# A gated cross-attention block with routed experts: the projections before the attention loop are derived in another way and spread differently over the engines

## The chip, the cores and the metric

The kernel runs on one core of a Trainium2 chip. The metric is the device time of one execution in microseconds (us); of several executions the median counts. The core has five engines with a queue each, which meet only at semaphores: PE (TensorE, products and transposes), DVE (VectorE), ACT (ScalarE), POOL (GpSimd) and SP (SyncE, which here only starts transfers). ACT and POOL start transfers too.

## The reference

`x` has 4 sequences of 1024 tokens of 256 values, the context has 77 keys for each sequence. Cut to what matters:

```python
def proj(x): return (x @ W1.T + b1) @ W2.T + b2
q  = proj(layernorm(x)); k = proj(ctx)
a  = softmax(q @ k.T / sqrt(256) + mask) @ ctx
x  = x + tanh(g_xattn) * a
h  = layernorm(x); route = softmax(h @ router_w + router_b)
e  = argmax(route)                       # one of 8 experts for each token
y  = (silu(h @ w1a[e]) * (h @ w1g[e])) @ w2[e]
x  = x + tanh(g_ffn) * max(route) * y
```

## The kernel before, in words

The tokens are taken in 8 groups (`NG`) of 4 x 128 (group g holds 128 tokens of each sequence, b = 0 to 3). There are three stages.

Preparation (to about 23 us). Both projections have no nonlinearity between their layers, so their product M = W2 W1 is formed once. `w2_t` is W2 transposed by PE (L973) and copied by DVE (L695). PE forms M transposed (`ps_p`, L993), which ACT copies to `m_t` (L541); `kp_t`, the projected keys, is M times the transposed context plus the bias `bq` (L1008; ACT adds the bias for one half at L553, DVE for the other at L720). The queries are never projected: the keys are multiplied by M once more (L1025, `keys_t`), so that the scores are raw tokens times `keys_t`. The layer norm's mean is taken off by using `m_c`, M with the mean over its input dimension removed. Before the change `m_c` is formed by a product of its own, W2 times the mean-free W1: DVE makes `w1_c` (L697 to L701), PE multiplies (L1014), DVE copies (L726). Then come `keys_t` (scaled by ACT at L556 and by DVE at L729), the bias row `bias_c` (product L1030, scaled by DVE at L732) and `values`, the context times tanh of the gate (DVE, L723). The norm's 1/deviation comes from `bn_stats` and `bn_aggr` on DVE (L687, L691: `stats1(g)`) and a power on POOL (L389, L390: `norm1`).

Attention loop. In round i each engine goes through a list written by hand: PE the scores of group i (L1049), the transposes of the tokens of group i+1 (L965), of the probabilities of group i-1 (L1039), and the attention products of group i-2 (L1058); ACT the copy of the transposed tokens (`copy_xt`, L548), the copy of the probabilities (L570), the exponentials (L579) and half a piece of expert 0's weights rounded to `w_hi` (L564); DVE mask and maximum (L749 to L755), the sum into `x_all` (L769), the second statistics (L778, L784) and `stats1(5 + i)` for i up to 2; POOL the masks (L400), `norm1`, `norm2` (L409 to L419) and the rest `w_lo` (L426). Then the tokens are sorted by expert (L812 to L1106), with a few unused products (L1104) among the PE work.

Expert loop (from about 96 us on). 36 tiles or so of 128 sorted tokens; PE multiplies with the weights split into two parts (L1127, L1137, L1145), three products each.

SP's queue: the weights, the context, 8 groups of `x`, then the three pieces of expert 0's weights into `staging`, piece k waiting until piece k-1 has landed (L328), then the rows of each finished group (L336), and so on. `m_t` and `m_c` share memory with `x_t[:, 1]`, which `copy_xt(1)` overwrites.

Of the kernel before, what the change touches and what calls it, by code (L numbers as in the profile page):

```python
# [20 lines left out]
ALU = mybir.AluOpType  # L21
# [3 lines left out]
P = 128  # L25


def flamingo_block(nc, x, ctx_kv, mask, g_xattn, g_ffn, w1, b1, w2, b2, router_w, router_b, e_w1, e_w2, out):
# [27 lines left out]
    UNUSED = (2, 2, 11)  # L56
    FIRST = 4
# [16 lines left out]
    with ExitStack() as top:  # L74
# [68 lines left out]
        w1_in, w2_in, w1_c, w2_t = (sb0(name, [P, DC, D]) for name in ("w1_in", "w2_in", "w1_c", "w2_t"))  # L143
        w1_mean = sb0("w1_mean", [P, 2, DC])
# [88 lines left out]
        w1c_step = sem("w1c_step")  # L233
# [12 lines left out]
        vr_ready = sem("vr_ready")  # L246
        bn1_ready = sem("bn1_ready")
# [62 lines left out]
        EARLY = 5  # L310
        QUARTERS = 4
# [7 lines left out]
        def _(sp):  # L319
# [36 lines left out]
        def _(pool):  # L356
# [28 lines left out]
            def norm1(first_group, end_group):  # L385
                n = (end_group - first_group) * B
                at = slice(first_group, end_group)
                pool.wait_ge(mv1_ready, end_group)
                link(nc.gpsimd.tensor_scalar(var_eps1[:, at], mv1[:, at, :, 1], EPS, None, ALU.add))  # L389
# [135 lines left out]
        def _(act):  # L525
# [13 lines left out]
            nc.scalar.activation(tanh_g[:], gates_in[:], ACT.Tanh).then_inc(tanh_ready, 1)  # L539
            act.wait_ge(m_psum, 1)  # L540
            nc.scalar.copy(m_t[:], ps_p[:].rearrange("p (c d) -> p c d", c=DC)).then_inc(mt_ready, 1)  # L541

            def copy_xt(g):
# [3 lines left out]
                for k in range(DC):  # L547
# [7 lines left out]
            act.wait_ge(keys_psum, 1)  # L555
            nc.scalar.mul(keys_t[:, 0, :, 0:KEYS], ps_p[:, 0:KB].rearrange("p (b k) -> p b k", b=B), SCALE  # L556
                          ).then_inc(keys_ready, 1)
# [123 lines left out]
        def _(dve):  # L681


            def stats1(g):
                dve.wait_ge(x_loaded[g], 16)
# [3 lines left out]
                dve.wait_ge(bn1_ready, g + 1)  # L689
                for b in range(B):  # L690
# [5 lines left out]
            dve.wait_ge(w1_loaded, 16)  # L696
            nc.vector.tensor_reduce(w1_mean[:, 0], w1_in[:], AX.X, ALU.add).then_inc(w1c_step, 1)  # L697
            dve.wait_ge(w1c_step, 1)
            nc.vector.tensor_scalar(w1_mean[:, 1], w1_mean[:, 0], 1.0 / D, None, ALU.mult).then_inc(w1c_step, 1)
            dve.wait_ge(w1c_step, 2)  # L700
            nc.vector.tensor_tensor(out=w1_c[:], in0=w1_in[:], in1=w1_mean[:, 1].unsqueeze(2).to_broadcast([P, DC, D]),  # L701
                                    op=ALU.subtract).then_inc(w1c_step, 1)
# [10 lines left out]
            stats1(1)  # L713
# [7 lines left out]
            dve.wait_ge(tanh_ready, 1)  # L721
            dve.wait_ge(ctx_loaded, 16)
# [5 lines left out]
            dve.wait_ge(keys_psum, 1)  # L728
            nc.vector.tensor_scalar(keys_t[:, 1, :, 0:KEYS], ps_o[1][:, 0:KB].rearrange("p (b k) -> p b k", b=B), SCALE,  # L729
                                    None, ALU.mult).then_inc(keys_ready, 1)  # L730
            dve.wait_ge(bias_psum, 1)
            nc.vector.tensor_scalar(bias_c[:], ps_s[1][:, 0:KB], SCALE, None, ALU.mult).then_inc(bias_ready, 1)  # L732
            stats1(4)

# [5 lines left out]
            def mask_and_max(g):  # L740
# [6 lines left out]
                dve.wait_ge(rstd1_ready, g + 1)  # L747
# [208 lines left out]
        def _(pe):  # L956
# [12 lines left out]
            pe.wait_ge(consts_ready, 1)  # L969
            pe.wait_ge(w2_loaded, 16)  # L970
# [4 lines left out]
            last.then_inc(w2t_psum, 1)  # L975
            pe.wait_ge(ctx_loaded, 16)
# [25 lines left out]

            for k in range(DC):
                pe.wait_ge(ctxt_ready[k], 1)
            pe.wait_ge(mt_ready, 1)
# [5 lines left out]
            pe.wait_ge(w1c_step, 3)  # L1011
# [15 lines left out]
            last.then_inc(keys_psum, 1)  # L1027
# [185 lines left out]
```

## Time and profile before

| | |
|---|---|
| three executions | 441.12, 441.44 (median), 442.80 us |
| the profiled execution | 444.54 us |
| its span, first to last instruction | 442.7 us |
| PE busy | 405.9 us (92%) |
| POOL busy | 241.8 us (55%) |
| DVE busy | 214.5 us (48%) |
| ACT busy | 180.6 us (41%) |

The profile is of one execution; its times count from the first instruction. A row of the timeline has the start, the duration of the group (from the start of its first to the end of its last instruction, both in us), the engine, the line, what is written and read, the shape and the number of instructions; in brackets how long the engine had been idle before and what ended that. The chain of waits is followed back from the last instruction. PE shows a float product as two instructions (two passes).

### The profile page before, as it was taken

What the parts mean: (1) busy time and instruction counts of PE and PEld (TensorE: products, weight loads), DVE (VectorE), ACT (ScalarE), POOL (GpSimd) and SP (SyncE); (2) the same over time, 40 slices, a digit from 0 to 9 for tenths busy, and PEclk for the clock granted to TensorE, in tenths of its full rate; (3) what the DMA queues carried; (4) which work ended last, traced back from release to release, by engine and by line L of the source; (5) the groups of instructions that cost most, each with busy time, mean ns of one, the idle gap of its engine ahead of it and who ended that gap; (6) DMA issues with size and microseconds to landing.
All of it is one profiled execution on the core that took longest, in us unless ns stands there. A gap on an engine that the chain in (4) does not pass through costs nothing.

```text
span 442.7 us, 9878 instructions
## 1 busy us (share of the span) xinstructions
PE 405.9 (92%) x2446; PEld 350.5 (79%) x2447; DVE 214.5 (48%) x520; ACT 180.6 (41%) x356; POOL 241.8 (55%) x323
## 2 busy tenths in 40 slices
PE   5998986289899999999999999999999999999990
PEld 4787874157788888888888888888888888888880
DVE  3789898934444434444334344334344434444340
ACT  1167654025443645445523245345433643233230
POOL 2356996224763787877772267738842686222231
PEclk9999895589999999999999999999999999999997
DMA  7941224825324243334440004423331000000100
GB/s 202 358 147 66 96 98 143 98 70 204 122 116 131 80 168 114 119 119 130 182 159 27 24 17 133 163 78 119 119 121 34 13 32 31 24 24 28 24 24 23
DMA packets 29850, 44.01 MB, mean 99 GB/s; under 512 B 8377, under 2 KB 25581, under 8 KB 27791
## 3 DMA queue, kind: packets, MB, share of 16 engines
q1 hardware_dynamic: 24095, 34.45, 23.9%
q0 software_dynamic: 3456, 9.11, 6.3%
q10 hardware_dynamic: 2288, 0.33, 0.5%
q8 instruction: 4, 0.07, 0.1%
q14 instruction: 7, 0.06, 0.0%
HBM read 35.44 MB, written 8.83 MB: 100 GB/s over the span
## 4 chain that ended last, share of the span: by engine, by line
PE 82%; POOL 6%; DVE 5%; DMA 2%; issue 2%; ACT 1%; DVEq 0%; POOLq 0%; SPq 0%; ACTq 0%
PE py L1145 22%; PE pa L1127 22%; PE pg L1127 22%; PE ph L1137 7%; POOL w_lo L426 2%; PE px L1112 2%; PE ps_s L1049 1%; PE ps_o L1058 1%; POOL rstd L410 1%; DMA ctx_in<-in_ctx 1%; PE ps_p L993 1%; PE ps_xt L965 1%; DVE x_norm L903 1%; DMA x_sorted<-residual_rows,idx_gather 1%; DVE x_all L769 1%
## 5 line engine op out<-in xcount | busy, mean ns | idle before, releaser
L920 DVE TENSOR_TENSOR ht_lo<-ph,ht_hi 128x512 fp32r<-128x512 f32 x70 | 48.4, 692 | 135.4 <-ACT ht_hi L651 135.4
L497 POOL TENSOR_TENSOR w_lo<-staging,w_hi x84 | 107.1, 1304 | 6.7 <-ACT w_hi L672 4.0
L651 ACT CAST ht_hi<-ph 128x512 fp32r<-128x512 f32 x70 | 41.1, 587 | 120.7 <-PE ph L1137 85.5
L1145 PE MATMUL py<-w_hi,ht_hi 128*128 x272 | 79.0, 291 | 0.0
L1145 PE MATMUL py<-w_lo,ht_hi 128*128 x272 | 76.2, 280 | 0.0
L1145 PE MATMUL py<-w_hi,ht_lo 128*128 x272 | 76.2, 280 | 0.0
L486 POOL DMA_INDIRECT out<-out_tile,idx_now x34 | 34.7, 1019 | 72.8 <-DVE out_tile L928 72.2
L1127 PE MATMUL pa<-w_hi,xt_hi 128*128 (+1 forms) x140 | 58.2, 416 | 0.8 <-ACT xt_hi L633 0.8
L453 POOL DMA_INDIRECT x_sorted<-residual_rows,idx_now x34 | 35.6, 1048 | 39.6 <-DVE x_norm L903 21.5
L1127 PE MATMUL pg<-w_lo,xt_hi 128*128 (+1 forms) x140 | 55.4, 396 | 0.0
L1127 PE MATMUL pg<-w_hi,xt_lo 128*128 (+1 forms) x140 | 55.4, 396 | 0.0
L1127 PE MATMUL pg<-w_hi,xt_hi 128*128 (+1 forms) x140 | 55.4, 395 | 0.0
L1127 PE MATMUL pa<-w_hi,xt_lo 128*128 (+1 forms) x140 | 55.3, 395 | 0.0
L1127 PE MATMUL pa<-w_lo,xt_hi 128*128 (+1 forms) x140 | 55.3, 395 | 0.0
L1145 PEld LDWEIGHTS py<-w_lo,ht_hi 128*128 128x128 f32 x272 | 52.0, 191 | 0.0
L915 DVE TENSOR_TENSOR hidden<-pg,silu 128x512 f32<-128x512 f32 x70 | 48.1, 686 | 6.6 <-ACT silu L645 3.4
L1145 PEld LDWEIGHTS py<-w_hi,ht_hi 128*128 128x128 f32 x272 | 51.1, 188 | 0.0
L1145 PEld LDWEIGHTS py<-w_hi,ht_lo 128*128 128x128 f32 x272 | 51.1, 188 | 0.0
L672 ACT CAST w_hi<-staging x21 | 40.1, 1912 | 9.8 <-PE py L1145 7.9
L645 ACT ACTIVATE silu<-pa 128x512 f32<-128x512 f32 x70 | 42.3, 604 | 1.9 <-PE pg L1127 1.9
L1137 PE MATMUL ph<-ident,hidden 128*128 128x128 f32 x280 | 41.9, 272 | 0.0
L633 ACT CAST xt_hi<-px 128x256 fp32r<-128x256 f32 x36 | 13.4, 372 | 59.2 <-PE px L1112 59.2
(185 smaller groups left out, 627.1 us busy)
## 6 DMA issues: line engine op xcount, KB each, us to landing
staging<-in_L_ffn_w SPq DMA_DIRECT2D x24, 1024.0 KB
residual_rows<-x_all SPq DMA_DIRECT2D x8, 516.0 KB, 3.7
x_all<-in_x SPq DMA_DIRECT2D x8, 512.0 KB, 10.2
x_sorted<-residual_rows,idx_now POOLq DMA_INDIRECT x34
out<-out_tile,idx_now POOLq DMA_INDIRECT x34, 2.5
w_in<-in_L_xattn_W SPq DMA_DIRECT2D x2, 256.0 KB, 4.6
ctx_in<-in_ctx SPq DMA_DIRECT2D x1, 308.0 KB
mask_in<-in_fside_1xSxS ACTq DMA_DIRECT2D x1, 308.0 KB, 11.0
```

The source lines that it names most:

```text
L453: pool.indirect_dma_start(x_sorted[:], None, rows, bass.IndirectOffsetOnAxis(ap=index, axis=0), bounds_check=last_row(t), oob_is_err=False ...
L486: pool.indirect_dma_start(out_rows, bass.IndirectOffsetOnAxis(ap=idx_now[:, 1:2], axis=0), tile_rows[:], None, bounds_check=limit, oob_is_ ...
L497: lo = nc.gpsimd.tensor_tensor(out=w_lo[:, bass.ds(dst + q * QW, QW)], in0=staging[:, bass.ds(src + q * QW, QW)], in1=w_hi[:, bass.ds(dst ...
L633: nc.scalar.copy(xt_hi[:], px[:, 0:D].rearrange("p (k n) -> p k n", k=DC)).then_inc(xhi_ready, 1)
L645: nc.scalar.activation(silu[:, j], pa[j][:], ACT.Silu).then_inc(silu_ready[j], 1)
L651: nc.scalar.copy(ht_hi[:, j], ph[j][:]).then_inc(hhi_ready[j], 1)
L672: nc.scalar.copy(w_hi[:, bass.ds(slot + src, PW)], staging[:, bass.ds(src, PW)]).then_inc(w_hi_ready, 1)
L915: nc.vector.tensor_tensor(out=hidden[:, j], in0=pg[j][:], in1=silu[:, j], op=ALU.mult).then_inc(hidden_ready[j], 1)
L920: nc.vector.tensor_tensor(out=ht_lo[:, j], in0=ph[j][:], in1=ht_hi[:, j].bitcast(FP32), op=ALU.subtract).then_inc(hlo_ready[j], 1)
L1127: last = mm(ps[:], xt[:, k], w[:, bass.ds(slot + (k * PW + col), HALF)], start=n == 0, stop=n == 3 * DC - 1)
L1137: last = nc.tensor.transpose(ph[j][:, c * P:(c + 1) * P], hidden[:, j, c * P:(c + 1) * P], ident[:])
L1145: last = mm(into[:, 0:D], ht[:, j, c * P:(c + 1) * P], w[:, bass.ds(slot + (DC * PW + (j * HC + c) * D), D)], start=j == 0 and n == 0, sto ...
```

## The change

- The product L1014 and DVE's work on W1 are gone. PE transposes `m_t` (4 transposes into the same PSUM tile), DVE takes mean and difference of that and writes `m_c`. The products for the projected keys now stand behind these transposes.
- ACT takes from DVE: `values`, the second half of `keys_t`, and `bias_c`. The product of `keys_t` signals for each half.
- ACT takes the first statistics of group 1: a sum over each row (4 instructions with accumulation), a scale, and a sum of squares (4 more), with `staging`'s third part as a place for results that nobody reads. POOL takes the variance from it. SP's transfer of piece 2 therefore waits for the squares. `stats1(1)` leaves DVE, and POOL's `norm1` runs in the order 0, 2, 3, then both masks, then 1, 4.
- On DVE `stats1(2)` moves behind `m_c` and `kp_t`.
- PE starts with 8 unused products of 128 x 128 before it waits for W2, and has one more behind W2's transposes.

```diff
+    UNUSED_EARLY = 8
+        X_ORDER = (0, 2, 3, 1, 4, 5, 6, 7)
@@ SP
+                if k == DC:
+                    sp.wait_ge(square_ready, 1)
@@ POOL
+                if first_group == 1:
+                    pool.wait_ge(square_ready, 1)
+                    link(nc.gpsimd.tensor_scalar(var_eps1[:, 1], x_square[:], 1.0 / D, EPS, ALU.mult, ALU.add))
-            for g in range(EARLY - 1):
+            for g in X_ORDER[:3]:
                 norm1(g, g + 1)
             mask1(0)
             mask1(1)
-            norm1(EARLY - 1, EARLY)
+            for g in X_ORDER[3:EARLY]:
+                norm1(g, g + 1)
@@ ACT
             nc.scalar.activation(tanh_g[:], gates_in[:], ACT.Tanh).then_inc(tanh_ready, 1)
+            act.wait_ge(ctx_loaded, 16)
+            act.wait_ge(tanh_ready, 1)
+            nc.scalar.activation(values[:, :, 0:D], ctx_in[:], ACT.Copy, scale=tanh_g[0:KEYS, 0:1]).then_inc(values_ready, 1)
             act.wait_ge(m_psum, 1)
             nc.scalar.copy(m_t[:], ps_p[:].rearrange("p (c d) -> p c d", c=DC)).then_inc(mt_ready, 1)
+            act.wait_ge(x_loaded[1], 16)
+            for b in range(B):
+                last = nc.scalar.activation(x_seen[:, b], x_all[:, 1, b, X0:KEPT], ACT.Copy, accum_out=x_sum[:, 0, b:b + 1])
+            last.then_inc(x_sum_step, 1)
...
             copy_xt(0)
+            for dc in range(DC):
+                act.wait_ge(keys_psum, dc + 1)
+                nc.scalar.mul(keys_t[:, dc, :, 0:KEYS],
+                              (ps_p, ps_o[1])[dc][:, 0:KB].rearrange("p (b k) -> p b k", b=B), SCALE).then_inc(keys_ready, 1)
+            act.wait_ge(bias_psum, 1)
+            nc.scalar.mul(bias_c[:], ps_s[1][:, 0:KB], SCALE).then_inc(bias_ready, 1)
+            act.wait_ge(x_sum_step, 1)
+            nc.scalar.mul(x_sum[:, 1], x_sum[:, 0], -1.0 / D).then_inc(x_sum_step, 1)
+            act.wait_ge(x_sum_step, 2)
+            for b in range(B):
+                last = nc.scalar.activation(x_seen[:, b], x_all[:, 1, b, X0:KEPT], ACT.Square, bias=x_sum[:, 1, b:b + 1],
+                                            accum_out=x_square[:, b:b + 1])
+            last.then_inc(square_ready, 1)
@@ DVE
-            stats1(1)
...
-            stats1(2)
+            dve.wait_ge(mc_psum, 1)
+            m_wide = ps_o[1][:].rearrange("p (c d) -> p c d", c=DC)
+            nc.vector.tensor_reduce(m_mean[:, 0], m_wide, AX.X, ALU.add).then_inc(mean_step, 1)
+            dve.wait_ge(mean_step, 1)
+            nc.vector.tensor_scalar(m_mean[:, 1], m_mean[:, 0], 1.0 / D, None, ALU.mult).then_inc(mean_step, 1)
+            dve.wait_ge(mean_step, 2)
+            nc.vector.tensor_tensor(out=m_c[:], in0=m_wide, in1=m_mean[:, 1].unsqueeze(2).to_broadcast([P, DC, D]),
+                                    op=ALU.subtract).then_inc(mc_ready, 1)
             dve.wait_ge(kp_psum, 1)
             nc.vector.tensor_scalar(kp_t[:, 1], ps_s[0][:, 0:KB], bq[:, 1:2], None, ALU.add).then_inc(kp_ready[1], 1)
-            nc.vector.tensor_scalar(values[:, :, 0:D], ctx_in[:], tanh_g[0:KEYS, 0:1], None, ALU.mult
-                                    ).then_inc(values_ready, 1)
-            dve.wait_ge(mc_psum, 1)
-            nc.vector.tensor_copy(m_c[:], ps_o[1][:].rearrange("p (c d) -> p c d", c=DC)).then_inc(mc_ready, 1)
+            stats1(2)
             stats1(3)
@@ PE
             pe.wait_ge(consts_ready, 1)
+            for _ in range(UNUSED_EARLY):
+                mm(ps_o[1][:, 0:P], ident[:], ident[:], start=True, stop=True)
             pe.wait_ge(w2_loaded, 16)
...
             last.then_inc(w2t_psum, 1)
+            mm(ps_o[1][:, 0:P], ident[:], ident[:], start=True, stop=True)
             pe.wait_ge(ctx_loaded, 16)
...
             last.then_inc(bq_psum, 1)
+            pe.wait_ge(mt_ready, 1)
+            for oc in range(DC):
+                for dc in range(DC):
+                    last = nc.tensor.transpose(ps_o[1][:, oc * D + dc * P:oc * D + (dc + 1) * P],
+                                               m_t[:, dc, oc * P:(oc + 1) * P], ident[:])
+            last.then_inc(mc_psum, 1)
...
-            for oc in range(DC):
-                for k in range(DC):
-                    last = mm(ps_o[1][:, oc * D:(oc + 1) * D], w2_t[:, k, oc * P:(oc + 1) * P], w1_c[:, k], start=k == 0,
-                              stop=k == DC - 1)
-            last.then_inc(mc_psum, 1)
```

## Rows read from the trace of the kernel before

**Rows 1.** The page, part 4: the chain that ended last, by line.

```profile
PE py L1145 22%; PE pa L1127 22%; PE pg L1127 22%; PE ph L1137 7%; POOL w_lo L426 2%; PE px L1112 2%; PE ps_s L1049 1%; PE ps_o L1058 1%; POOL rstd L410 1%; DMA ctx_in<-in_ctx 1%; PE ps_p L993 1%; PE ps_xt L965 1%; DVE x_norm L903 1%; DMA x_sorted<-residual_rows,idx_gather 1%; DVE x_all L769 1%
```

**Rows 2.** Chain of waits, first 75 us: start us, us, what, instructions.

```profile
8.65 3.61 PE ps_p L993 x8
12.26 1.50 PE ps_o L999 x8
13.76 2.26 PE ps_o L1008 x4
16.02 1.37 PE ps_s L1008 x4
17.39 1.73 PE ps_o L1014 x8
19.11 0.87 PE ps_xt L965 x8
...
23.34 1.75 PE ps_s L1049 x16
...
26.00 1.08 ACT x_t L548 x2
```

**Rows 3.** Windows: stretch, us, busy of PE, PEld, DVE, ACT, POOL, granted clock, DMA.

```profile
40.00:45.00 5.00, 3.33 (x20) 2.82 (x18) 4.89 (x20) 3.03 (x11) 4.09 (x9) 0.89 0.02 5
45.00:50.00 5.00, 4.81 (x25) 4.20 (x25) 3.17 (x15) 2.50 (x9) 4.76 (x9) 0.77 0.32 107
```

**Rows 4.** Timeline of PE.

```profile
4.74 1.09 PE L973 MATMUL ps_o<-ident,w_in 128*128 128x128 f32 x4 [4.74 <-DMA w_in<-in_L_xattn_W]
...
45.60 1.86 PE L965 MATMUL ps_xt<-ident,x_all 128*128 128x128 f32 x8
...
96.24 0.47 PE L1127 MATMUL pa<-w_hi,xt_hi 128*128 128x512 f32 x1 [0.55 <-ACT xt_hi L633]
```

**Rows 5.** Timeline of ACT.

```profile
9.76 0.20 ACT L539 ACTIVATE tanh_g<-gates_in 128x2 f32<-128x2 f32 x1 [1.57 <-DMA gates_in<-in_g_ffn]
12.30 0.59 ACT L541 COPY x_t<-ps_p 128x512 f32<-128x512 f32 x1 [2.33 <-PE ps_p L993]
...
22.34 0.43 ACT L556 ACTIVATE keys_t<-ps_p 128x308 f32<-128x308 f32 x1 [1.24 <-PE ps_o L1025]
...
28.34 1.04 ACT L564 CAST w_hi<-staging 128x1024 fp32r<-128x1024 f32 x1
```

**Rows 6.** Timeline of DVE.

```profile
7.23 0.69 DVE L697 TENSOR_REDUCE w_mean<-w_in 128x2 f32<-128x512 f32 x1 [0.67 <-DMA w_in<-in_L_xattn_W]
...
11.93 1.41 DVE L687 BATCH_NORM_STATS2 bn<-x_all 128x6 f32<-128x256 f32 x4 [0.37 <-DMA x_all<-in_x]
...
17.88 0.74 DVE L723 TENSOR_SCALAR values<-ctx_in,tanh_g 77x1024 f32<-77x1024 f32 x1
...
25.50 0.88 DVE L749 SCALAR_TENSOR_TENSOR masked<-ps_s,rstd,mask_c 128x77 f32<-128x77 f32 x4
```

**Rows 7.** Instructions of L600 and L608: duration in ns, min/median/max.

```profile
L600 ACT ACTIVATE ps_s<-x_all x4: 367/378/388, 69.2 to 73.1; 128x256 f32<-128x256 f32 x4
...
L608 ACT ACTIVATE mask_c<-x_all,mean_bias x2: 492/500/508, 70.4 to 70.9; 128x256 f32<-128x256 f32 x2
```

**Rows 8.** Timeline of SP's queue: the three pieces of expert 0's weights.

```profile
14.15 10.12 SPq L331 DMA_DIRECT2D staging<-in_L_ffn_w  x2
30.45 0.38 SPq L333 DMA_DIRECT2D staging<-in_L_ffn_w  x1
```

**Rows 9.** Timeline of POOL.

```profile
21.97 1.03 POOL L390 TENSOR_TENSOR rstd<-var_eps,minus_half 128x4 f32<-128x4 f32 x1
24.01 1.52 POOL L400 TENSOR_TENSOR mask_c<-bias_c,mask_in 128x308 f32<-128x308 f32 x2 [1.01 <-DVE bias_c L732]
...
40.59 0.23 POOL L389 TENSOR_SCALAR var_eps<-mv 128x4 f32<-128x4 f32 x1 [3.68 <-DVE mv L691]
```

**Rows 10.** Waits, 60 to 96 us: engine, line, waited for, us in total, times, longest.

```profile
DVE x_all L769 <- PE ps_o L1058: 0.5, 1, 0.5
```

More of the change, by code:

```diff
@@ L142, in flamingo_block @@
         ctx_in = sb0("ctx_in", [KEYS, B, D])
-        w1_in, w2_in, w1_c, w2_t = (sb0(name, [P, DC, D]) for name in ("w1_in", "w2_in", "w1_c", "w2_t"))
-        w1_mean = sb0("w1_mean", [P, 2, DC])
+        w1_in, w2_in, w2_t = (sb0(name, [P, DC, D]) for name in ("w1_in", "w2_in", "w2_t"))
+        m_mean = sb0("m_mean", [P, 2, DC])
+        x_seen = staging[:, DC * PW:DC * PW + B * D].rearrange("p (b d) -> p b d", b=B)
+        x_sum = sb0("x_sum", [P, 2, B])
+        x_square = sb0("x_square", [P, B])
         ctx_t = sb0("ctx_t", [P, DC, KB])
@@ L232, in flamingo_block @@
         router_c_ready = sem("router_c_ready")
-        w1c_step = sem("w1c_step")
+        mean_step = sem("mean_step")
+        x_sum_step = sem("x_sum_step")
         m_psum = sem("m_psum")
@@ L246, in flamingo_block @@
         vr_ready = sem("vr_ready")
+        square_ready = sem("square_ready")
         bn1_ready = sem("bn1_ready")
@@ L387, in norm1 @@
                 at = slice(first_group, end_group)
-                pool.wait_ge(mv1_ready, end_group)
-                link(nc.gpsimd.tensor_scalar(var_eps1[:, at], mv1[:, at, :, 1], EPS, None, ALU.add))
+                if first_group == 1:
+                    pool.wait_ge(square_ready, 1)
+                    link(nc.gpsimd.tensor_scalar(var_eps1[:, 1], x_square[:], 1.0 / D, EPS, ALU.mult, ALU.add))
+                else:
+                    pool.wait_ge(mv1_ready, end_group if end_group == 1 else end_group - 1)
+                    link(nc.gpsimd.tensor_scalar(var_eps1[:, at], mv1[:, at, :, 1], EPS, None, ALU.add))
                 nc.gpsimd.tensor_tensor(out=rstd1[:, at], in0=var_eps1[:, at],
@@ L554, in _ @@
             copy_xt(0)
-            act.wait_ge(keys_psum, 1)
-            nc.scalar.mul(keys_t[:, 0, :, 0:KEYS], ps_p[:, 0:KB].rearrange("p (b k) -> p b k", b=B), SCALE
-                          ).then_inc(keys_ready, 1)
+            for dc in range(DC):
[11 more added lines that the diff above has]
+            last.then_inc(square_ready, 1)
             def high0(c):
@@ L684, in stats1 @@
             def stats1(g):
+                n = g + 1 if g < 1 else g
                 dve.wait_ge(x_loaded[g], 16)
@@ L688, in stats1 @@
                 last.then_inc(bn1_ready, 1)
-                dve.wait_ge(bn1_ready, g + 1)
+                dve.wait_ge(bn1_ready, n)
                 for b in range(B):
@@ L695, in _ @@
             nc.vector.tensor_copy(w2_t[:], ps_o[0][:].rearrange("p (c d) -> p c d", c=DC)).then_inc(w2t_ready, 1)
[L696 to L702, printed above, removed]
             dve.wait_ge(ctxt_psum, 1)
@@ L717, in _ @@
             nc.vector.tensor_copy(bq_wide[:], bq[:].unsqueeze(2).to_broadcast([P, DC, P])).then_inc(bq_step, 1)
-            stats1(2)
+            dve.wait_ge(mc_psum, 1)
[6 more added lines that the diff above has]
+                                    op=ALU.subtract).then_inc(mc_ready, 1)
             dve.wait_ge(kp_psum, 1)
             nc.vector.tensor_scalar(kp_t[:, 1], ps_s[0][:, 0:KB], bq[:, 1:2], None, ALU.add).then_inc(kp_ready[1], 1)
-            dve.wait_ge(tanh_ready, 1)
-            dve.wait_ge(ctx_loaded, 16)
-            nc.vector.tensor_scalar(values[:, :, 0:D], ctx_in[:], tanh_g[0:KEYS, 0:1], None, ALU.mult
-                                    ).then_inc(values_ready, 1)
-            dve.wait_ge(mc_psum, 1)
-            nc.vector.tensor_copy(m_c[:], ps_o[1][:].rearrange("p (c d) -> p c d", c=DC)).then_inc(mc_ready, 1)
-            stats1(3)
[L728 to L732, printed above, removed]
+            stats1(2)
+            stats1(3)
             stats1(4)
@@ L746, in mask_and_max @@
                     dve.wait_ge(probs_ready, g - 1)
-                dve.wait_ge(rstd1_ready, g + 1)
+                dve.wait_ge(rstd1_ready, X_ORDER.index(g) + 1)
                 for b in range(B):
@@ L1001, in _ @@
             last.then_inc(bq_psum, 1)
+            pe.wait_ge(mt_ready, 1)
[4 more added lines that the diff above has]
+            last.then_inc(mc_psum, 1)
             for k in range(DC):
                 pe.wait_ge(ctxt_ready[k], 1)
-            pe.wait_ge(mt_ready, 1)
             for oc in range(DC):
@@ L1026, in _ @@
                               stop=k == DC - 1)
-            last.then_inc(keys_psum, 1)
+                last.then_inc(keys_psum, 1)
             pe.wait_ge(bq_step, 2)
```

1 line of the change is left out of this document (removed).

## The prediction

> **What bounds the kernel now.** I read the chain of waits by line first [rows 1]: nearly four fifths of it are PE's products of the expert loop (L1145, L1127, L1137), which the change doesn't touch. So the change can only move the moment at which that loop starts. The chain in order of time then shows what sets this moment [rows 2]: from 6.4 to 25 us it is one unbroken run of PE instructions, each starting where the last one ends. PE is the bound of the preparation, and each microsecond by which scores(0) (L1049, at 23.34) comes earlier is a candidate. DVE is close behind: its last `stats1(4)` ends just when it takes the first mask at 25.50 [rows 6], against PE's end of scores(0) at 23.34 + 1.75 = 25.1. PE alone would therefore win only some 0.4 us; the change takes both off.
>
> The durations hold the second finding. L993 and L1014 are the same work, eight instructions of 256 columns, and took 3.61 and 1.73 us; the two halves of L1008 took 2.26 and 1.37 [rows 2]. So PE ran at 1.2 GHz until some time within the second half of L1008, about 16.6 us, and at 2.4 GHz from there (the granted clock is given as 1.00 in these first rows, but the durations say otherwise). Half speed costs about 1.8 us in L993 and 1.2 in the first half of L1008.
>
> **The change, part by part.** I follow the new order with the old durations. "Fast" and "slow" are the two levels.
>
> *Head of PE.* The identity is ready at about 1.6 us, W2 lands at 4.74 [rows 4]. Eight products of 128 columns are 16 instructions; a slow instruction of 128 columns took 1.86 / 8 = 0.23 us [rows 4], so they end at about 5.3 and push W2's transposes back by 0.6 us; the ninth takes 0.5 in the wait for the context. This delay is covered: L993 also needs W1, which lands at 7.2 [rows 6], and the real cover stands further on, at `m_t`. What the trace of before doesn't show is what they do to the clock. PE would be at work from 1.6 us with hardly a gap, where it began at 4.7 and was fast at 16.6. Bounds: no effect (the fast level at 16.6 as before), or fast by 5 to 9 us. I take the second. The nearest rows are those of a later slow stretch [rows 3]: a mean of 0.89 over 40 to 45 us is 1.1 us at 0.50, a mean of 0.77 over 45 to 50 is 2.3 us, so the slow level came at 43.9 and went at 47.3. PE did scores and then eight transposes through it without a gap [rows 4], dense work of the kind that the head of the kernel now gets. The long slow stretch up to 16.6, in contrast, held L999 (1.50 us for products of one column [rows 2]) and pauses for landings.
>
> *To `m_t`.* With the context's transposes and the small router product at either level, L993 starts at about 8.4 and ends, fast, near 10.2. Its copy waits for ACT, which has a new entry ahead of it: `values`. Tanh cannot start before 9.76 [rows 5], so `values` runs from 9.97; 1024 elements took ACT 1.04 [rows 5], so it ends at 11.0, and `m_t` (0.59 [rows 5]) at 11.7. ACT's queue, not PE, sets this point: about 0.9 us of the faster PE is lost here, and a rise of the clock at any time up to 9 us gives the same result.
>
> *`m_c`.* Four fast transposes, half of L965's 0.87 [rows 2], end at 12.2. DVE's chain (0.69 [rows 6] for the reduction, 0.2, 0.69 for the difference, which reads PSUM; I take the same duration, between 0.5 and 1.0) ends at 13.9 and is hidden beside the two products for `kp_t`, which at the fast level take 2.08 (half of 2.05 + 2.05 slow, or two of 1.04). They end at 14.3. L1014, 1.73 us, is gone. From L965 to scores(0) the old chain took 23.34 - 19.11 = 4.23 us [rows 2], all fast, with the same products; so scores(0) starts at 18.5 instead of 23.34, 4.8 us earlier.
>
> *ACT behind it.* The sums of group 1 need `x` group 1, landed at 11.9 [rows 6]; four at 0.42 each (0.38 [rows 7] and a little) end at 13.7, before `kp_t` wants ACT at 14.3. `keys_t` costs 0.43 on ACT against 0.48 on DVE [rows 5, 6]; here the second half is ready at 17.7, before PE has finished L1030 at 18.5. Then `bias_c` to 18.95, the scale to 19.2, four squares at 0.51 [rows 7] to 21.3. Behind them in the queue waits `copy_xt(1)`, the head of the chain at 26.00 [rows 2]; its transposes end at 18.5 + 1.75 + 0.9 = 21.15. So it starts at 21.3: the squares cost 0.1 us, and the gain is 4.7. Each further 0.1 us for the eight passes would cost the same here.
>
> *DVE and POOL.* DVE is free at 14.9, does three groups of statistics at 1.8 (1.41 [rows 6] and 0.4 for the aggregates) and ends at 20.3; group 4 has landed by then (about 1.65 us a group). POOL's `norm1(3)` then runs from 18.5 to 19.8 (1.03 [rows 9] and 0.3), and the mask, at 0.76 [rows 9], is ready at 20.6. The first mask operation on DVE moves from 25.50 [rows 6] to 20.6 or 20.7: 4.8 earlier, set by POOL now. `norm1(1)` follows both masks and the squares and ends at 22.8; its reader, the mask of group 1, comes at 24.4.
>
> *Transfers.* They don't move with the rest, so they might be late next. Piece 0 had landed before SP issued piece 1, which was done at 14.15 + 10.12 = 24.3; piece 1 had landed by 30.45 [rows 8]. ACT's first use of piece 0 (28.34 [rows 5]) moves to 23.6, that of piece 1 comes two rounds later, near 32. The margins are about 1 us and 1.8 us. The new wait on the squares (21.3) ends long before piece 2 may be issued at 30.45; behind it in SP's queue stand only the row stores from 44 us on. POOL was idle for 3.68 us before its work at 40.59 [rows 9], waiting for DVE, so it can follow too. Nothing absolute is left that would hold the loop back, and the rest shifts as a whole.
>
> **The skill against the rows.** For products the new order uses ScalarE where the Trainium skill (ScalarE: Activation LUTs, "Rules for kernel authors") says to use VectorE. The rows agree for `values`: 0.74 on DVE [rows 6] against 1.04 for as many elements on ACT [rows 5], and its place ahead of `m_t` makes it worse; left on DVE it would let `m_t` start at 10.2, and the sum would be 0.9 higher. The Trainium skill (TensorE: Matmul & The Clock Gate, Part 1) warns that the number of slow matmuls at the start of a kernel varies from run to run; by that the gain would scatter, which one profile can't show.
>
> **The rivals.** (B) The unused products don't bring the fast level earlier. For it: PE was busy for ten microseconds before the clock rose. Slow, the steps give: W2's transposes to 6.2, L993 from 8.8 to 12.4, L999 to 13.9 (1.50 [rows 2]), transposes of `m_t` to 14.8, the `kp_t` products slow to 16.6 and fast for the rest, to 17.8; scores(0) at 22.0. Gain 1.3 us, 440.1. (C) The clock rises early but falls again, in the pause of PE before `m_t` (about 10.9 to 11.7), or the shifted schedule puts a slow stretch on the first expert tile. Slow stretches of 3.4 us do occur [rows 3]; each costs half of itself where PE is the bound, 1.7 us: gain 3.0, 438.4. Against it: PE's pause is short, where in 40 to 45 us PE was idle for 5.00 - 3.33 = 1.7 us ahead of the fall [rows 3]. (E) Slower than before: B, and in the gap ahead of the first expert tile, whose first product started at 96.24 [rows 4], the clock falls and stays low for two such stretches; the tiles then lose 3.4 us, which beats the gain of 1.3: 443.5. It decides from a loss above 1.3 us and needs two unlikely things.
>
> **The numbers.** The profiled execution took 444.54 us, 442.7 of it its span; the gain is a difference within it, and I take it off the median of 441.44: 441.44 - 4.7 = 436.7 (a span of 438.0). Chances: forecast 0.60, B 0.14, C 0.22, E 0.04. Something of 0.5%, 2.2 us, is about what a measurement can tell from no change, so the line lies at 439.2: faster 0.82 (forecast and C), same 0.14 (B), slower 0.04. Low end: in the slow part around 70 us DVE waited 0.5 us for PE [rows 10], which another position of the slow stretches would save, and `values` or the copies may be some tenths cheaper, and DVE's difference is hidden whatever it takes between its bounds: 435.4. High end: B with a little on top, 440.2.
>
> **What would show it.** In the profile of the changed kernel: L993 near 1.8 us in place of 3.61; ACT's `values` right behind tanh, ending near 11.0, with `m_t` right behind; scores(0) at 18.5; `copy_xt(1)` released by ACT's own squares at about 21.3; DVE's first mask at 20.7, released by POOL; the first expert product at 91.5 instead of 96.24. L993 still at 3.6 would mean B. A mask or a copy waiting for a landing would mean that a transfer I called hidden is not.

## The result, and the profile after

The changed kernel is 2% slower, where I had forecast faster.

| | before | after |
|---|---|---|
| median | 441.47 us (441.12 to 442.80, 6 executions) | 452.31 us (450.03 to 455.59, 6 executions) |
| ratio after / before | | 1.020 [1.016, 1.024] |
| profiled execution | 444.54 us | 451.63 us |
| its span | 442.7 us | 449.6 us |
| first expert product starts | 96.24 us [rows 4] | 91.41 us |
| from there to the end of the span | 346.5 us | 358.2 us |

The last two lines tell nearly all. In these two profiles the preparation won 4.8 us, as I had forecast (4.7), and the expert loop, which the change doesn't touch, lost 11.7 us. (442.7 - 96.24 = 346.5; 449.6 - 91.41 = 358.2.) The medians lie 10.8 us apart and the two profiled executions 7.1: that of before was 3.1 us slower than its median. This comes back in the part on why the prediction was wrong.

The preparation first. The timeline of PE of the changed kernel answers to [rows 2]:

```profile
1.57 3.41 PE L995 MATMUL ps_o<-ident 128*128 128x128 f32 x16 [1.57 <-POOL ident L375]
4.82 0.60 PE L999 MATMUL ps_o<-ident,w_in 128*128 128x128 f32 x4
...
8.11 1.97 PE L1020 MATMUL ps_p<-w_t,w_in 128*128 128x256 f32 x8
...
11.41 0.66 PE L1033 MATMUL ps_o<-ident,x_t 128*128 128x128 f32 x4 [0.54 <-ACT x_t L558]
...
18.00 1.91 PE L1075 MATMUL ps_s<-keys_t,x_t 128*128 128x85 f32 x16
...
91.41 0.47 PE L1153 MATMUL pa<-w_hi,xt_hi 128*128 128x512 f32 x1 [0.55 <-ACT xt_hi L666]
```

W2's four transposes take 0.60 us where they took 1.09 [rows 4], L1020 (L993 of before) 1.97 instead of 3.76 (3.61 in the chain of [rows 2]), so PE is at its fast level by about 5 us; scores(0) starts at 18.00 instead of 23.18 (the same row of the timeline of before; 23.34 in the chain), 5.2 us earlier. On ACT and DVE:

```profile
9.74 1.15 ACT L556 ACTIVATE values<-ctx_in,tanh_g 77x1024 f32<-77x1024 f32 x1
10.79 0.56 ACT L558 COPY x_t<-ps_p 128x512 f32<-128x512 f32 x1
...
20.65 0.19 ACT L588 ACTIVATION_READ_ACCUMULATOR staging<-x_all,x_sum 128x1 f32 x1
20.83 1.07 ACT L570 COPY x_t<-ps_xt 128x512 f32<-128x512 f32 x2
...
24.38 1.05 ACT L597 CAST w_hi<-staging 128x1024 fp32r<-128x1024 f32 x1 [1.00 <-DMA staging<-in_L_ffn_w]
...
20.44 0.91 DVE L773 SCALAR_TENSOR_TENSOR masked<-ps_s,rstd,mask_c 128x77 f32<-128x77 f32 x4 [0.59 <-PE ps_s L1075]
```

Now the loop. The chain that ended last, by line, of the changed kernel; `x_norm`, which had 1% in [rows 1], is now fifth with 5%:

```profile
PE py L1171 21%; PE pg L1153 17%; PE pa L1153 17%; PE ph L1163 7%; DVE x_norm L927 5%; PE px L1138 3%; SPq L332 2%; DMA staging<-in_L_ffn_w 2%; ACT ht_hi L684 2%; DVE x_all L793 2%; PE ps_s L1075 1%; POOL w_lo L439 1%; DVE bn L802 1%; POOL rstd L423 1%; DMA x_sorted<-residual_rows,idx_gather 1%
```

`x_norm` is DVE's instruction in `norm(t + 1)`: it normalizes the gathered rows of the next tile, PE transposes them (`px`), and PE's products of that tile wait for this. Its durations (minimum, median, maximum in ns) and first and last start, before and then after:

```profile
L903 DVE TENSOR_SCALAR x_norm<-x_sorted x36: 404/408/1981, 94.8 to 424.0; 128x256 f32<-128x256 f32 x36
```

```profile
L927 DVE TENSOR_SCALAR x_norm<-x_sorted x36: 403/551/1621, 89.9 to 431.0; 128x256 f32<-128x256 f32 x36
```

PE's waits for it (us in total, times, longest), before and after:

```profile
PE px L1112 <- DVE x_norm L903: 3.5, 3, 1.7
```

```profile
PE px L1138 <- DVE x_norm L927: 13.3, 16, 1.8
```

The same instruction on the same 256 columns takes 0.41 us at its best in both. From its first to its last start it is 329.2 us before and 341.0 after, 11.8 more. After, 14 of the 36 take 1.47 us or more; before, one does. The difference of 13, at 0.9 us each (the distance of neighbouring starts is 9.5 us without and 10.4 with a long `x_norm`), is 11.7 us.

What holds it stands in one tile of the two timelines. Before (DVE, then GpSimd, called POOL):

```profile
156.76 0.69 DVE L920 TENSOR_TENSOR ht_lo<-ph,ht_hi 128x512 fp32r<-128x512 f32 x1 [3.06 <-ACT ht_hi L651]
157.36 0.68 DVE L915 TENSOR_TENSOR hidden<-pg,silu 128x512 f32<-128x512 f32 x1
157.96 0.41 DVE L903 TENSOR_SCALAR x_norm<-x_sorted 128x256 f32<-128x256 f32 x1
...
155.64 5.12 POOL L497 TENSOR_TENSOR w_lo<-staging,w_hi  x4
```

After:

```profile
153.20 0.69 DVE L944 TENSOR_TENSOR ht_lo<-ph,ht_hi 128x512 fp32r<-128x512 f32 x1 [3.06 <-ACT ht_hi L684]
153.87 0.69 DVE L939 TENSOR_TENSOR hidden<-pg,silu 128x512 f32<-128x512 f32 x1
154.48 1.54 DVE L927 TENSOR_SCALAR x_norm<-x_sorted 128x256 f32<-128x256 f32 x1
...
152.08 5.07 POOL L511 TENSOR_TENSOR w_lo<-staging,w_hi  x4
```

GpSimd computes the low parts of the next expert's weights, `w_lo`, in four quarters of 1.27 us each (5.07 / 4). Count from its start: borders between quarters at 1.27, 2.54 and 3.81 us. Before, `x_norm` starts at 157.96 - 155.64 = 2.32 and ends at 2.73, just behind the second border. After, it starts at 2.40 and ends at 3.94, just behind the third. Where it starts earlier, 2.06 us behind the first quarter (before) or 2.13 (after), it takes 0.63 or 0.55 us and also ends near 2.7. So a running quarter holds `x_norm` until its end, and an `x_norm` that starts 0.08 us later misses one border and waits a whole quarter for the next. Which of the two comes next at a border isn't decided by the recorded start alone: the fourth `x_norm` of before starts at 3.22 us and ends only at 5.20, two borders later, while in a later run (`b_body1`) the one of the same tile starts at 3.23 and ends at 3.92. `hidden` and `ht_lo`, which have an input in PSUM, run through the quarters in 0.69 us; they are also another operation than `x_norm`, and no run separates the two reasons.

The Trainium skill (GPSIMD Engine Reference, "Specifications") says that GpSimd shares its SBUF interfaces with VectorE, with contention for VectorE instructions in a two-port performance mode or with two inputs in SBUF. The hold agrees if `x_norm`, which has one SBUF tensor as input, runs in such a mode, which no row shows. That the wait lasts to the end of a whole GpSimd instruction is what the rows show.

And the 0.08 us: `hidden` is the first DVE instruction of the loop's body. It starts 157.36 - 156.76 = 0.60 us behind the last instruction of the round before, `ht_lo`, in the kernel before, and 0.67 in the changed one. This holds from the sixth `x_norm` on in every tile, also where GpSimd has no weights to work on. The body of the loop is the same. What differs is how many instructions DVE has ahead of it: 13 fewer, counting one wait.

### The profile page after: what moved, and what is told of

Its sections match the earlier page's. It is cut to its first block, busy times and chain, and to the rows that moved or that the text cites. A ratio compares the mean times of both kernels' runs of the same rounds, so it can differ in the third digit from the quotient of the medians.

```text
span 449.6 us, 9914 instructions
## 1 busy us (share of the span) xinstructions
PE 403.1 (90%) x2460; PEld 346.7 (77%) x2461; DVE 226.7 (50%) x508; ACT 185.8 (41%) x376; POOL 240.9 (54%) x323
## 4 chain that ended last, share of the span: by engine, by line
PE 68%; DVE 12%; issue 5%; DMA 4%; POOL 3%; ACT 3%; SPq 3%; DVEq 1%; POOLq 0%; ACTq 0%
PE py L1171 21%; PE pg L1153 17%; PE pa L1153 17%; PE ph L1163 7%; DVE x_norm L927 5%; PE px L1138 3%; SPq L332 2%; DMA staging<-in_L_ffn_w 2%; ACT ht_hi L684 2%; DVE x_all L793 2%; PE ps_s L1075 1%; POOL w_lo L439 1%; DVE bn L802 1%; POOL rstd L423 1%; DMA x_sorted<-residual_rows,idx_gather 1%
## 6 DMA issues: line engine op xcount, KB each, us to landing
x_all<-in_x SPq DMA_DIRECT2D x8, 512.0 KB, 10.1
```

## The experiments

Two theories, one on top of the other. **L**: the loss is `x_norm` held for a whole quarter; whatever changes the meeting of the two takes it away. **P**: the late start of `hidden` comes from the place of the loop in DVE's instruction stream. The rivals: another effect of the change in the loop, of the memory layout, of the unused products, or of one chip. "Restored" below means that no `x_norm` of the steady loop is held for a whole quarter of 1.27 us any more.

**The place, with 13 instructions put back.** 13 memsets of one column at DVE's head, in its idle time, ahead of the first wait:

```diff
+            for j in range(13):
+                nc.vector.memset(pad[:, j:j + 1], 0.0)
             dve.wait_ge(w2t_psum, 1)
```

> The changed kernel with 13 tiny memsets at the head of VectorE's queue, where it is idle until 5.5 us; VectorE's expert loop then starts at the same place of its instruction stream as in the kernel before. Theory P (place of VectorE's loop): the 0.07 us by which the first product of each tile (hidden) starts later after the loop's branch is due to the place of the loop in the stream. Then hidden follows ht_lo by 0.60 us again instead of 0.67, x_norm is 0.41 us and not 1.5 in the tiles with weights, and the kernel takes 441.4 - 4.8 = 436.6 us. Rival S (a phase carried in from the earlier start, or the place of another engine's loop): nothing changes, 450 to 455 us, hidden 0.67 behind.

Measured: 441.49 us, ratio to before 0.995 [0.992, 0.999]. In its timeline the tile looks as before:

```profile
152.49 0.69 DVE L947 TENSOR_TENSOR ht_lo<-ph,ht_hi 128x512 fp32r<-128x512 f32 x1 [3.06 <-ACT ht_hi L685]
153.10 0.68 DVE L942 TENSOR_TENSOR hidden<-pg,silu 128x512 f32<-128x512 f32 x1
153.70 0.41 DVE L930 TENSOR_SCALAR x_norm<-x_sorted 128x256 f32<-128x256 f32 x1
...
151.37 5.12 POOL L512 TENSOR_TENSOR w_lo<-staging,w_hi  x4
```

Thirteen instructions that do nothing, more than 80 us ahead of the loop, take the span from 449.6 to 438.4 us. That is P's result in the loop. The time that I had expected, 436.6 us, was missed by 4.9; the part on why the prediction was wrong says where they lie.

**The counterpart on the kernel before**, with 3 of them, to stand like the changed kernel if places counted by sixteens:

> The kernel before with 3 tiny memsets at the head of VectorE's queue, which puts its loop 16 instructions behind the place that it has in the changed kernel. Theory P, if what matters is the place within a block of 16 or fewer: the kernel before becomes slow without the change, x_norm near 1.5 us in most tiles with weights, 441.4 + 11 = 452 us. Rival S: 441.4 us as before.

Measured: 442.41 us, ratio 0.998 [0.994, 1.001], `hidden` at 0.61, `x_norm` 0.41. So not by sixteens.

**Shorter quarters.** The changed kernel, place left as it is, and the same edit in the kernel before:

```diff
-        QUARTERS = 4
+        QUARTERS = 8
```

> The changed kernel with GpSimd's subtraction for w_lo in 8 instructions of 256 columns for each piece instead of 4 of 512. Theory L (x_norm cannot start while one of these instructions runs, and waits for its end): x_norm waits for at most 0.65 us instead of 1.27, so it ends before PE wants it or at most 0.2 us later; 436.5 to 439 us. Rival M (x_norm is slow for another reason, such as its own memory or the gather): x_norm stays at 1.5 us and the time at 450 to 455 us.

> The kernel before with 8 instructions for each piece instead of 4, the control of the run before: 441 to 443 us under both theories; the difference to the changed kernel with the same edit should be the 4.8 us of the preparation.

Measured: changed kernel 440.13 us, ratio 0.991 [0.988, 0.995]; kernel before 443.00, ratio 0.999 [0.996, 1.002]. The distance is 2.9 us and not the expected 4.8, and 440.13 lies above the expected 436.5 to 439. In the changed one `hidden` is still late (0.67), and `x_norm` takes 0.55 to 0.61 us in 13 of the 21 tiles with weights, 0.92 at most:

```profile
151.33 0.69 DVE L944 TENSOR_TENSOR ht_lo<-ph,ht_hi 128x512 fp32r<-128x512 f32 x1 [3.06 <-ACT ht_hi L684]
152.00 0.69 DVE L939 TENSOR_TENSOR hidden<-pg,silu 128x512 f32<-128x512 f32 x1
152.61 0.59 DVE L927 TENSOR_SCALAR x_norm<-x_sorted 128x256 f32<-128x256 f32 x1
...
150.22 5.67 POOL L511 TENSOR_TENSOR w_lo<-staging,w_hi  x8
```

and PE's waits for it:

```profile
PE px L1138 <- DVE x_norm L927: 2.5, 2, 1.7
```

This is the run that carries L: the late start alone costs nothing that the measurement can tell, and the hold is the loss. The eight pieces together take 5.67 us where four took 5.07 to 5.12, which GpSimd has room for.

**Both.** If the place had cost something beside the hold, the two remedies would add:

> The changed kernel with both edits, the 13 tiny memsets on VectorE and GpSimd's subtraction in 8 instructions. If theory P (place of VectorE's loop) and theory L (x_norm waits for the end of a GpSimd instruction) name the same loss, the two don't add up: about 440 us, within 0.7 us of either alone, with the first product of a tile 0.61 us behind ht_lo and no x_norm over 1 us after the third tile. If they are separate losses, they add: 438.5 us or less.

Measured: 440.18 us, ratio 0.993 [0.990, 0.996], against 440.13 with the quarters alone. They don't add; it is one loss.

**The parts of the change.** The restored kernel without the nine unused products, and the kernel before with them alone:

> The padded changed kernel without the 9 unused products at PE's head. Theory C (they bring PE's fast level forward): L993's counterpart takes 3.6 us instead of 1.9, scores(0) starts near 21 us and not at 18, and the whole is 2 to 3.5 us slower than with them. Rival N (the gain at the head comes from the product that was removed and from the work moved off VectorE): scores(0) within 1 us of 18 and the time within 1 us of the padded kernel.

> The kernel before with the 9 unused products alone. Theory C with VectorE as the next bound: L993 takes about 1.9 us, scores(0) starts near 21 us, and VectorE's first mask operation, which was at 25.5, at 23 to 23.5: 2 to 2.5 us less than the kernel before. Rival V (VectorE holds the start whatever PE does): first mask operation at 25 or later, within 0.5 us of the kernel before.

Measured: 442.66 us, ratio 1.000 [0.997, 1.004], and 442.76 us, ratio 0.999 [0.996, 1.003]. In the first, L1022 (L993 of before) is slow again and scores(0) a microsecond later than with them; in the second, L996 is fast, but PE then waits for DVE:

```profile
8.25 3.53 PE L1022 MATMUL ps_p<-w_t,w_in 128*128 128x256 f32 x8
...
19.05 1.91 PE L1077 MATMUL ps_s<-keys_t,x_t 128*128 128x85 f32 x16
```

```profile
8.11 1.97 PE L996 MATMUL ps_p<-w_t,w_in 128*128 128x256 f32 x8
...
17.25 1.27 PE L1028 MATMUL ps_p<-kp_t,x_t 128*128 128x308 f32 x4 [1.49 <-DVE x_t L726]
...
20.43 1.91 PE L1052 MATMUL ps_s<-keys_t,x_t 128*128 128x85 f32 x16
```

Neither half alone moves the time by more than the measurement can tell. The two together, with the loop restored, do so in three runs of four (0.995, 0.991 and 0.993, intervals below 1; the fourth, `a_pad3_r` below, reaches 1.000), by less than 1%. The expectations were missed in part: in the first, scores(0) came at 19.05 where I had expected 21 (its time is 2.5 us above that of both remedies on the same chip, as expected), and the second was 0.6 us faster than the kernel before on its chip, not 2 to 2.5, although its first mask came at 22.76. The first expert product at 92.15 and 93.49 in these two profiles doesn't decide it either: in the profiles of the kernel before with edits elsewhere it lies between 92.91 and 96.23.

**Does it repeat?** The changed kernel once more:

> The changed kernel itself, untouched, beside the others of this call. Theory P (the number of VectorE instructions ahead of its loop sets, in every tile, how late the first VectorE instruction behind the branch starts, and the 0.07 us so lost push x_norm into a running w_lo quarter): it repeats, 450 to 455 us, hidden 0.67 us behind ht_lo, x_norm 1.5 us in most tiles with weights. Rival, chance of one chip or build: 439 to 444 us here, hidden 0.61.

Measured: 449.42 us (446.59 to 450.65) against 443.50 on that chip, ratio 1.012 [1.005, 1.020]; `hidden` 0.67 behind `ht_lo`, `x_norm` at 1.47 us or more in 14 tiles. It repeats, 0.6 us below what I expected. It isn't one chip: on the chip of this run and on that of `a_tail3` below, both the slow loop and a restored one are on record.

**Which stream.** The same 13 small instructions on ACT instead of DVE:

> The changed kernel with 13 tiny copies at the head of ScalarE's stream in place of the 13 tiny memsets that restored it on VectorE. Theory P wants VectorE's own stream shifted, so nothing changes: hidden 0.67 us behind ht_lo, x_norm 1.5 us in most tiles with weights, 450 to 455 us. Rival (any disturbance at the head, or another memory layout by the extra buffer, restores it): hidden 0.61, x_norm 0.41, 439 to 444 us.

Measured: 449.60 us (one execution), `hidden` at 0.67, PE's waits for `x_norm` 12.2 us. Neither another buffer in memory nor a disturbance at the head restores it; DVE's own stream has to shift.

**How much of a shift, and where.** In the changed kernel 3 memsets at DVE's head, one execution and then ten on the chip of `after_again`:

> The changed kernel with 3 memsets instead of 13, one look at the loop. If the place of the loop matters only by whether it is that of the kernel before, hidden stays 0.67 us behind ht_lo and x_norm at 1.5 us. If any shift restores it, 0.61 and 0.41.

> The changed kernel with 3 tiny memsets at VectorE's head, timed in rounds. Theory P: three instructions are enough to leave the bad place, hidden 0.61 us behind ht_lo, x_norm 0.41 us, and the time is that of the one with 13, 439 to 442 us, ratio to the kernel before 0.990 to 0.998. Rival (its single look was a lucky one): 443 or more, ratio 1.00 or above.

Measured: 439.27 us, and 440.65 us, ratio 0.996 [0.992, 1.000]; against the unrestored kernel on the same chip that is 8.8 us less. 1 and 16 of them at the head, and 3 behind the loop in place of ahead of it, one execution each:

> The changed kernel with 1 tiny memset at VectorE's head. If only some residues of the loop's place are bad, this tells how narrow the bad one is: a single bad place gives hidden 0.61 and 439 to 444 us; a bad stretch of two or more gives 0.67 and 448 to 454 us.

> The changed kernel with 16 tiny memsets at VectorE's head. If the place of the loop counts by blocks of 16 instructions (or of 8), nothing changes: hidden 0.67, x_norm 1.5 us, 448 to 454 us. If by longer blocks or by something else: hidden 0.61, x_norm 0.41, 439 to 444 us.

> The changed kernel with the 3 tiny memsets behind VectorE's loop in place of ahead of it. Theory P (the place of the loop in VectorE's stream): nothing changes, hidden 0.67 us behind ht_lo, x_norm 1.5 us in most tiles with weights, 448 to 454 us. Rival (the length of the whole stream, or where it is put in memory as a whole): hidden 0.61, x_norm 0.41, 439 to 444 us.

Measured: 439.57 us with 1 (`hidden` 0.61, `x_norm` 0.41), 441.14 with 16 (the same), 451.53 with 3 behind the loop (0.67; 1.5 us). So it is how many instructions stand ahead of the loop, not the length of the stream, and one is enough. And at a distance of 64, in either kernel, one execution each:

> The kernel before with 51 tiny memsets at VectorE's head, 3 to 4 us of work that lies in its idle time there. Its loop then stands 64 instructions behind where it stands in the changed kernel. If the place counts by blocks of 16, 32 or 64 instructions: hidden 0.67 us behind ht_lo, x_norm 1.5 us in most tiles with weights, about 450 to 456 us. If by something else (another length of block, the code's bytes, the place together with another engine's): hidden 0.61, x_norm 0.41, 440 to 446 us.

> The changed kernel with 64 tiny memsets at VectorE's head: the loop stands exactly 64 instructions behind its bad place. If the place counts by blocks of 64 instructions: hidden 0.67, x_norm 1.5 us, 448 to 456 us. If by something else: hidden 0.61, x_norm 0.41, 439 to 446 us. (1, 3, 13 and 16 more instructions have all restored it.)

Measured: 439.86 and 440.89 us, both with `hidden` at 0.61. Places 1, 3, 13, 16 and 64 behind the bad one are all good. I found no second bad place, and so never made the kernel before slow.

**Where the time goes.** The chain also names VectorE's own queue (`DVEq`: register, branch and wait instructions), and "issue" is time in which nothing that the profile shows is waited for. At the moment at which VectorE enters the loop in the changed kernel, and then with 1 memset at its head:

```profile
113.46 0.05 DVEq L974
113.51 0.41 issue
113.92 0.02 DVEq L938
```

```profile
114.07 0.05 DVEq L977
114.12 0.39 issue
114.50 0.05 DVEq L977
```

L974 here (L977 with the memset) is the loop's own first instruction, L938 the first of its body. One more instruction ahead of the loop puts the pause one instruction earlier, out of the loop; with 3 (`a_pad3`) it stands three instructions earlier than in the changed kernel (0.39 us at 113.67); in the kernel before and in `a_pad13` there is none at this point, and VectorE goes from the one to the other in 0.05. So there is a point in VectorE's stream that costs 0.4 us when it is first crossed, and in the changed kernel it falls between the first and the second instruction of the loop. There it costs in every round, as in the one shown above:

```profile
153.29 0.06 DVEq L974
153.35 0.25 issue
153.60 0.05 DVEq L974
```

The first row is the loop's branch. From its end to the body's first instruction it is 0.45 us in the five profiles with `hidden` at 0.67 and 0.24 in the fifteen others. Of these 0.21 us, 0.07 are seen in `hidden`; the rest passes while `ht_lo` still runs.

**A failed test of L.** To delay `x_norm` alone, in the kernel before, a memset between `hidden` and `x_norm` in the loop's body, first of 1 column, then of 128:

```diff
                 multiply(t, 0, start)
+                nc.vector.memset(pad[:, 0:1], 0.0)
                 norm(t + 1)
```

> The kernel before with one tiny memset between hidden and x_norm in VectorE's loop body: x_norm starts some 0.06 us later behind the first w_lo quarter, as in the changed kernel, and nothing else is touched. Theory (x_norm just misses the border between two quarters and is held for a whole one, and this alone is the loss): x_norm 1.5 us in about 15 tiles, 450 to 455 us, ratio 1.015 to 1.03. Rival (the late start of hidden itself, or another effect of the place, costs the time): x_norm stays near 0.41 us or costs nothing on the path, 441 to 445 us.

> The kernel before with a memset of 128 columns between hidden and x_norm in VectorE's loop body. The one of a single column (b_body1) delayed nothing: x_norm still started 0.60 us behind hidden. This one should hold VectorE some 0.1 to 0.2 us (estimate from x_norm's 0.41 us for 256 columns), and only that is changed. Theory (x_norm is held for the rest of a quarter of w_lo when it misses a border, and this is the loss): x_norm starts 2.4 to 2.5 us behind the first quarter and takes 1.4 to 1.5 us, in about 15 tiles, 449 to 455 us, ratio 1.01 to 1.03. Rival (the late start of hidden is the cause, x_norm's hold is its companion): x_norm's delay costs at most itself, 24 tiles x 0.15 = 3.6 us, 441 to 446 us.

Measured: 443.01 us, ratio 0.997 [0.994, 1.000], and 442.95, ratio 0.998 [0.995, 1.001]. Of the second:

```profile
157.94 0.68 DVE L916 TENSOR_TENSOR hidden<-pg,silu 128x512 f32<-128x512 f32 x1
158.60 0.17 DVE L935 MEMSET pad<- 128x128 f32 x1
158.68 0.28 DVE L904 TENSOR_SCALAR x_norm<-x_sorted 128x256 f32<-128x256 f32 x1
...
156.22 5.12 POOL L498 TENSOR_TENSOR w_lo<-staging,w_hi  x4
```

The memset of 128 columns moved `x_norm`'s start by 0.14 us (2.46 behind `w_lo` instead of 2.32) and shortened it by 0.13: it ends 2.74 us behind the start of `w_lo`, where it ended at 2.73 without. Its start in the record is earlier than the moment at which it needs what GpSimd has, and that moment wasn't moved. The edit didn't make the delay, so this says nothing for or against L; L rests on the runs with eight pieces.

## Why the prediction was wrong

**Right, step by step.** The unused products end at 4.98 (forecast 5.3) and bring the fast level; L1020 ends at 10.1 (10.2); `values` ends at 10.9 (11.0), `m_t` at 11.35 (11.7), the transposes at 12.1 (12.2), `m_c` at 13.7 (13.9); scores(0) starts at 18.00 (18.5); ACT's squares end at 20.84 (21.3) and release `copy_xt(1)`; DVE's first mask starts at 20.44 (20.7); the first expert product at 91.41 (91.5). Rival B fell with L1020, and E with it. Of C, the pause ahead of `m_t` did no harm in this profile; with 1 and with 16 memsets PE paused there for 1.32 and 1.46 us, the granted clock was 0.50 from 11.9 to 15.3, and scores(0) came at 20.2. A slow stretch on the first expert tile occurs too, in three restored kernels (93.3 to 96.7 us without unused products, 91.4 to 94.8 with both remedies, 91.5 to 94.9 with 64 memsets), but not in the profile of the changed one.

**Misses in it.** The four lines of PE that I called nearly four fifths of the chain are 73% of it; nothing hangs on this. The row of the first mask names PE as what ended the wait. But scores(0) was done at 19.91, and POOL's first mask at about 20.3 (two of them took 1.52 us from 19.55), so the forecast that POOL sets this moment holds. The first weight piece, however, wasn't hidden: ACT waited 1.00 us for its landing at 24.38. I had given it a margin of about 1 us, and my own row allowed a landing as late as 24.3, behind the first use at 23.6. This was my sign of a transfer that isn't hidden, and in the changed kernel the chain of the preparation runs through it:

```profile
13.76 10.60 DMA staging<-in_L_ffn_w
...
25.33 0.24 ACT x_t L570
```

Until then the new order was 5.2 us ahead (scores(0) at 18.00 against 23.18, scores(1) at 22.05 against 27.22); from the copy at 25.33 on it is 4.8 (scores(2) at 26.45 against 31.24). That 4.8 was forecast is therefore partly luck: scores(0) came 0.5 us earlier than forecast, and the landing took 0.4 back.

**The step that failed** is the last one of the parts: "Nothing absolute is left that would hold the loop back, and the rest shifts as a whole." I had looked for absolute times, the transfers, and found none (the first weight piece was one, for 0.4 us). The loop was moved as a whole, but it wasn't the same inside: `x_norm` met the quarters of `w_lo` 0.08 us later, and this cost 11.7 us. The trace of before held half of this. One `x_norm` of 1.98 us against a median of 0.41, and ends at 2.7 us behind `w_lo` whatever the start, would have shown that the loop runs close to a border, and that missing one costs about a microsecond a tile (the tile with the 1.98 took 10.75 us, the later ones 9.51). No view of before could show that 13 fewer instructions ahead of a loop make its first instruction 0.07 us later. So the loss was not to be forecast, but a rival "the loop's fit with GpSimd is lost" could have stood there; with the 13 tiles of 0.9 us that were measured since it gives 441.4 - 4.7 + 11.7 = 448.4, on the right side of the kernel before.

**A size that was off too.** Where the loop is restored, the gain is 1.6 us (441.49 with 13 memsets against 443.11 on the same chip) to 3.2 (440.18 with both remedies against 443.37), not 4.7. The term is the subtraction: I took a gain within one profiled execution, 444.54 us, off the median of others. The profiled one was slow just where the gain arises, at the head and in the middle. Windows of the kernel before, around the two slow stretches of the middle (the column ahead of the last two is the granted clock):

```profile
35.00:50.00 15.00, 13.14 (x80) 11.58 (x79) 12.83 (x49) 9.48 (x32) 10.75 (x19) 0.89 0.12 41
65.00:95.00 30.00, 16.14 (x72) 10.71 (x72) 23.73 (x81) 7.49 (x31) 12.29 (x25) 0.60 0.51 111
```

The same of the kernel before with 51 memsets, whose first `x_norm` starts at 91.5 instead of 94.8:

```profile
35.00:50.00 15.00, 11.49 (x86) 10.27 (x86) 12.97 (x50) 8.85 (x25) 10.94 (x18) 1.00 0.21 73
65.00:95.00 30.00, 14.13 (x78) 9.79 (x77) 22.08 (x78) 7.92 (x25) 11.09 (x23) 0.77 0.45 109
```

A mean of 0.89 over 15 us is 3.3 us at the slow level, 0.60 over 30 us is 24 us; in the second kernel it is none and 14. The rise at the head moves too: in the seven profiles without unused products it came at 11.4 to 12.4 us in three and at 16.4 to 17.2 in four, before (16.6) among them. With 51 memsets it came at 12.4, and scores(0) started at 21.08 instead of 23.18. So of the 3.3 us by which its first `x_norm` is earlier, 2.1 come from the head and 1.2 from the rest, and the preparation of before, which those memsets leave alone, must take some 3 us less in some executions too; this is argued from one profile, not measured on before itself. The Trainium skill (TensorE: Matmul & The Clock Gate, Part 1) says that the number of slow matmuls at the start varies from run to run; these profiles agree. With this term put right, at the ratios of 0.991 to 0.996 that the four restored kernels with the whole change show, and no loss in the loop, the median would have been 437.6 to 439.8, inside my range; with the loop's 11.7 us on top of a gain of 3.2 to 1.6 it comes to 450.0 to 451.6, against 452.31 measured.

**What stays open.** What the point in VectorE's stream is that costs 0.4 us at first and 0.2 in every round. That the number of instructions ahead of the loop decides is shown in the changed kernel; in the kernel before, the bad place (13 fewer) was never reached. The Trainium skill (Advanced Engine Details and Errata, "ISA Cache") says that a line of the instruction cache holds 256 instructions and that there are two of them; a loop cut by the border of such a line would fit a single bad place that 64 doesn't repeat, but no run here shows it. And that a delay of `x_norm` alone, with nothing else changed, brings the loss was tried twice and not achieved.

## What to carry to other kernels

When a change shortens what stands ahead of a loop, compare the loop in the two traces instruction by instruction, by offsets from a common event: a loop that isn't touched can still run in another rhythm, and here that was worth more than twice the gain. If a VectorE instruction that others wait for shares SBUF with GpSimd work, cut the GpSimd work into pieces shorter than the slack: with eight pieces the changed kernel has the lowest median of those timed repeatedly, 440.13 us, at its bad place (440.18 with both remedies, not to be told apart). And take a gain that hangs on the clock's slow stretches from several profiles, not from one.

## What the runs showed of the hardware

- A VectorE instruction with SBUF in and out (`x_norm`, 256 columns, 0.41 us) waits for the end of the running GpSimd tensor instruction, now and then of the next one too: 1.5 us instead of 0.41 in most of the held tiles, 2.02 at most (`a_pad64`). The wait is on record as a longer instruction, not as idle time. A `tensor_tensor` with an input in PSUM (`hidden`, 0.69 us) doesn't wait.
- The same loop of VectorE starts its first instruction 0.60 or 0.67 us behind the last one of the round before, by how many instructions stand ahead of the loop; one more was enough to change it. The trace shows a pause at a fixed point of VectorE's stream, 0.41 us when it is first crossed, and a way of 0.45 us instead of 0.24 from the branch to the body when the point lies inside the loop.
- A VectorE instruction of up to 128 columns put between two others of a dense sequence can cost nothing: the next one's record starts later and is shorter by as much (0.28 in place of 0.41 us).
- The clock's rise at the head of the kernel came at 4.4 to 7.8 us with unused products and at 11.4 to 17.2 us without, and the slow stretch within 65 to 95 us took 14 us in one execution and 24 in another.
